# The inverse and the solve of a chunked recurrence, on 64x64 diagonal tiles of TensorE instead of zero-padded full rows

## The reference

```
for t in range(45):
    b_t = kk_t * a_t
    sa  = -S @ kk_t
    S   = S * dec_t[None, :] + outer(sa, b_t) + outer(v_t, k_t)
    o_t = S @ r_t
```

## Time and profile before

| | us |
|---|---|
| median of 3 runs | 312.54 |
| range of the runs | 311.07 to 313.73 |
| the profiled execution, its time | 310.39 |
| its span, first to last instruction | 308.6 |
| PE busy | 281.8 |
| ACT busy | 200.1 |
| DVE busy | 189.0 |
| POOL busy | 127.5 |

### The profile page before, as it was taken

The page is one execution under the profiler, slowest core; times in us unless marked ns, Lnnn a source line. Parts: engine busy times, 40 slices in busy tenths (PEclk is TensorE's granted clock), DMA queues, the critical chain, the costliest instruction groups (busy, mean ns, idle before and its releaser), DMA issues.

```text
span 308.6 us, 13595 instructions
## 1 busy us (share of the span) xinstructions
PE 281.8 (91%) x5880; PEld 214.8 (70%) x5880; DVE 189.0 (61%) x346; ACT 200.1 (65%) x356; POOL 127.5 (41%) x122
## 2 busy tenths in 40 slices
PE   3999789999999999999777886999999999999996
PEld 1557567888975666766443474887989888976785
DVE  5258878899347763424797988789765655244202
ACT  1587983555575978787998976294865326666541
POOL 9006899131040066666346159674378200021000
PEclk9999999999995999999999979999999999999999
DMA  7932221222212222221200000000000000000002
GB/s 237 415 87 62 66 57 54 62 63 63 64 54 57 62 54 63 60 62 56 62 24 0 2 2 2 2 5 4 4 4 4 4 4 5 4 4 2 2 26 74
DMA packets 20563, 14.99 MB, mean 49 GB/s; under 512 B 2328, under 2 KB 19352, under 8 KB 20376
## 3 DMA queue, kind: packets, MB, share of 16 engines
q1 hardware_dynamic: 20504, 14.13, 14.7%
HBM read 13.38 MB, written 0.74 MB: 46 GB/s over the span
## 4 chain that ended last, share of the span: by engine, by line
PE 68%; ACT 21%; DVE 6%; POOL 3%; issue 2%; DVEq 0%; POOLq 0%
PE PS L772 62%; PE PS L884 5%; ACT L342 3%; ACT arena L372 3%; ACT arena L368 2%; ACT arena L366 2%; ACT arena L407 2%; DVE PS L510 1%; ACT arena L415 1%; ACT arena L381 1%; DVE arena L670 1%; ACT arena L358 1%; POOL arena L322 1%; ACT arena L419 1%; POOL arena L326 1%
## 5 line engine op out<-in xcount | busy, mean ns | idle before, releaser
L772 PE MATMUL PS<-arena,K 64*64 64x180 f32 (+3 forms) x1296 | 132.0, 372 | 14.3 <-DVE PS L510 5.3
L772 PEld LDWEIGHTS PS<-arena,K 128*64 128x64 f32 (+2 forms) x1296 | 74.6, 145 | 55.2 <-issue 21.1
L772 PE MATMUL PS<-arena 128*45 128x45 f32 (+5 forms) x3584 | 108.1, 222 | 5.0 <-POOL arena L315 2.6
L772 PEld LDWEIGHTS PS<-arena 128*45 128x45 f32 (+3 forms) x3584 | 98.9, 125 | 18.9 <-issue 5.1
L305 POOL TENSOR_TENSOR arena<-arena 128x360 f32<-128x360 f32 x32 | 29.8, 958 | 37.8 <-DVE arena L684 37.8
L684 DVE TENSOR_TENSOR arena<-PS,arena 128x360 f32<-128x360 f32 x32 | 16.8, 531 | 23.0 <-PE PS L772 20.0
L407 ACT ACTIVATE arena<-PS,K 128x720 f32<-128x720 f32 x32 | 25.2, 861 | 2.4 <-PE PS L772 1.8
L281 POOL TENSOR_TENSOR WG<-WG,K 128x2048 f32<-128x2048 f32 x4 | 15.2, 3814 | 25.6 <-DMA WG<-wr 25.6
L559 DVE TENSOR_TENSOR arena<-PS,arena 128x360 f32<-128x360 f32 x20 | 10.6, 531 | 22.0 <-ACT arena L368 22.0
L389 ACT COPY arena<-PS 128x720 f32<-128x720 f32 x16 | 12.4, 775 | 15.4 <-PE PS L884 15.2
L772 PE MATMUL PS<-K,arena 128*45 128x64 f32 (+4 forms) x472 | 19.3, 230 | 1.9 <-DVE arena L737 0.9
(11 more groups left out here) (125 smaller groups left out, 375.3 us busy)
## 6 DMA issues: line engine op xcount, KB each, us to landing
WG<-wr SPq DMA_DIRECT2D x64, 64.0 KB, 1.9
arena<-wr SPq DMA_DIRECT2D x64, 64.0 KB, 1.8
arena<-xT SPq DMA_DIRECT2D x4, 368.0 KB, 5.0
K<-consts SPq DMA_DIRECT2D x1, 1171.0 KB, 10.2
K<-consts SPq DMA_DIRECT2D x1, 852.0 KB, 8.0
out<-arena SPq DMA_DIRECT2D x4, 180.0 KB, 1.9
K<-consts SPq DMA_DIRECT2D x1, 510.0 KB, 6.0
K<-consts SPq DMA_DIRECT2D x1, 352.0 KB, 6.8
```

The costliest lines, as they stand in the source:

```text
L772: return nc.tensor.matmul(o, l, r, start=start, stop=stop)
```

## The change

- The matmuls of `lx`, `lt`, `u`, `y2`, `o` read only the 45 rows of their own sequence, on partitions 64j to 64j+44, for both operands; `z` reads 32 rows and `w` 13 (from partition 64j+32).
- The zeroed copies go, with their waits (`ltb`, `ttb`, `lt32`, `sab`): all of ACT's share of `m`, of the last `lt` and of `w`, one of ACT's two copies in `vt`, DVE's second operation in `w`. `lx` writes 360 elements a row.
- The ones beside V are written by POOL at the outset, in two small memsets for each chunk, each behind a wait on POOL's own semaphore; ACT's and DVE's copies in `v` go.
- `TABLE` is another order of the same steps, from the first to the last. Parts of it, old and new, are shown.
- The constants lose 187 columns of 128.

```diff
@@ the table, attention's start @@
-mean.1:2 q.0:0 var.1:12 mean.1:3 k.0:0 q.0:12 var.1:3 kx.0:0 k.0:1 v.0:0 q.0:3 kx.0:1 k.0:2 v.0:1 k.0:3 kx.0:2 v.0:2
-kx.0:3 v.0:3 s.0:01 e.0:0 s.0:23 e.0:1 t.0:0 e.0:2 t.0:1 pv.0:0 t.0:2 pv.0:1 e.0:3 s.1:01 t.0:3 e.1:0 pv.0:23 t.1:0
+var.1:12 mean.1:3 k.0:0 q.0:1 var.1:3 q.0:2 kx.0:0 k.0:1 kx.0:1 q.0:3 k.0:23 v.0:0 kx.0:2 v.0:1 s.0:0 e.0:0 v.0:2
+kx.0:3 s.0:1 t.0:0 e.0:1 v.0:3 s.0:2 pv.0:0 t.0:1 s.0:3 pv.0:1 s.1:01 e.0:2 e.1:0 e.0:3 e.1:1 t.0:2 t.1:0 t.0:3 pv.1:0
@@ the table, from the first kb on @@
-ab.0:0 mean.3:3 aw.0:1 gh.0:0 ab.0:1 gg.0:0 gh.0:1 kk.0:0 gg.0:1 kk.0:1 bon.0:0 kb.0:0 bon.0:1 var.3:3 vw.0:2
-mixes.0:3 m.0:0 aw.0:2 m.1:0 kb.0:1 rk.0:3 vt.0:0 ab.0:2 vw.0:3 lx.0:0 m.0:1 lt.0:0 aw.0:3 lx.1:0 m.1:1 gh.0:2 lt.1:0
...
-lx.1:2 vt.0:3 o.0:0 lt.1:2 mean.4:0 lx.0:3 u.0:1 var.4:0 lt.0:3 lx.2:2 y2.0:1 lx.1:3 lt.2:2 lt.1:3 lx.3:2 z.0:1 lx.2:3
-lt.3:2 lt.2:3 ro.0:0 u.0:2 lx.3:3 w.0:1 mean.5:0 y2.0:2 lt.3:3 z.0:2 o.0:1 u.0:3 w.0:2 var.5:0 y2.0:3 mean.4:1 o.0:2
-var.4:1 z.0:3 mean.4:2 f.0:0 w.0:3 var.4:2 r.0:0 o.0:3 ro.0:12 mean.4:3 mean.5:12 var.4:3 var.5:12 r.1:0 ro.0:3 f.0:1
+rk.0:1 vw.0:01 aw.0:0 mixes.0:2 cb.7:3 aw.0:1 ab.0:0 y.7:3 rk.0:2 ab.0:1 gh.0:01 gg.0:0 kk.0:0 gg.0:1 kk.0:1 bon.0:0
+kb.0:0 mean.3:3 bon.0:1 kb.0:1 var.3:3 vw.0:2 m.0:01 mixes.0:3 aw.0:2 m.1:0 rk.0:3 ab.0:2 m.1:1 vt.0:0 gh.0:2 vw.0:3
...
+w.0:1 ro.0:0 lt.1:3 mean.5:0 lx.2:23 o.0:1 var.5:0 mean.4:1 lt.2:23 f.0:0 lx.3:23 lt.3:23 var.4:1 u.0:23 y2.0:23
+z.0:23 w.0:23 o.0:23 mean.4:2 ro.0:1 var.4:2 mean.4:3 mean.5:1 r.0:0 var.4:3 var.5:1 ro.0:2 r.1:0 mean.5:2 f.0:1
@@ GpSimd, for each chunk @@
                 g.memset(a(c, VD_, PP * 2 * NKV * 18), 0.0).then_inc(sem["init"], 1)
+                pool.wait_ge(sem["init"], 3 * c + 1)
+                for hh in range(2):
+                    if hh:
+                        pool.wait_ge(sem["init"], 3 * c + 2)
+                    ones = a(c, VD_, PP * 2 * NKV * 18, 64 * hh, 64 * hh + T).rearrange("q (x u) -> q x u", u=18)
+                    g.memset(ones[:, :, 9 * hh + HD], 1.0).then_inc(sem["init"], 1)
+                pool.wait_ge(sem["init"], 3 * c + 3)
@@ ScalarE @@
-                    s.copy(ones, vec("tok")[64:128, :].broadcast_to([64, PP * 2 * NKV]))
-                elif name == "m":
-                    act.wait_ge(sem["m_ev"], n)
-                    p0, p1 = i * PP // 2, (i + 1) * PP // 2
-                    for j in range(2):
-                        last = s.activation(pair(a(c, LT_[j]))[:, p0:p1], m2(c)[:, p0:p1], ACT.Copy, scale=vec(f"tok{j}"))
-                    last.then_inc(sem["ltb"], 1)
-                    for j in range(2):
-                        last = s.activation(a(c, VT_[j], 512), bank(c, 0, 512), ACT.Copy, scale=vec(f"tok{j}"))
-                    last.then_inc(sem["vt"], 1)
+                    s.copy(a(c, VT_, 512), bank(c, 0, 512)).then_inc(sem["vt"], 1)
-                elif name == "lt" and i == len(LEVELS) - 1:
-                    act.wait_ge(sem["t_ev"], n)
-                    for j in range(2):
-                        last = s.activation(pair(a(c, TB_[j])), ...)
-                    last.then_inc(sem["ttb"], 1)
-                    for j in range(2):
-                        last = s.activation(pair(a(c, LT_[j])), m2(c), ACT.Copy, scale=vec(f"early{j}"))
-                    last.then_inc(sem["lt32"], 1)
-                    s.activation(a(c, U_, 512), bank(c, 0, 512), ACT.Copy, scale=k("row32")).then_inc(sem["z_ev"], 1)
-                elif name == "w":
-                    act.wait_ge(sem["sa"], 2 * n - 1)
-                    s.activation(a(c, SA_[0], 512), a(c, Y_, 512), ACT.Copy, scale=vec("tok0")).then_inc(sem["sab"], 1)
+                    s.copy(a(c, U_, 512), bank(c, 0, 512)).then_inc(sem["z_ev"], 1)
@@ VectorE @@
-                    v.tensor_tensor(x.rearrange("q j (p t) -> q j p t", t=T),
-                                    pair(bank(c, 0)).unsqueeze(1).broadcast_to([128, 2, PP, T]),
-                                    level.unsqueeze(2).broadcast_to([128, 2, PP, T]), ALU.mult).then_inc(sem["x_ev"], 1)
+                    v.tensor_tensor(pair(a(c, X_)), pair(bank(c, 0)), over_pairs(k("levels", i * T, (i + 1) * T)),
+                                    ALU.mult).then_inc(sem["x_ev"], 1)
-                    dve.wait_ge(sem["sa"], 2 * n - 1)
-                    v.tensor_scalar(a(c, SA_[1], 512), a(c, Y_, 512), vec("tok1"), None, ALU.mult).then_inc(sem["sa"], 1)
@@ TensorE @@
+            def seq(j, lo=0, hi=T):
+                return 64 * j + lo, 64 * j + hi
-                        last = mm(to_bank(c, 0, T, j, p, T), a(c, LT_[j] + p * T, T), tt(c, p, 0))
+                        last = mm(to_bank(c, 0, T, j, p, T), m4(c, p, 2, seq(j)), tt(c, p, 0, seq(j)))
...
+                        early = seq(j, 0, 32)
+                        last = mm(to_bank(c, 0, D, j, p, T), m4(c, p, 2, early), a(c, Y_ + p * D, D, *early))
...
+                        late = seq(j, 32, T)
+                        last = mm(to_bank(c, 1, D, j, p, T), tt(c, p, 1, late), a(c, U_ + p * D, D, *late))
```

More of the change, by code:

```diff
@@ L26 @@
 GROUPS = [
-    [("tokA", 64), ("tokB", 64), ("mean", 128), ("cent", 128), ("vecs", 36)],
+    [("tokA", 64), ("tokB", 64), ("mean", 128), ("cent", 128), ("vecs", 30)],
     [("wq", 128), ("wqr", 128), ("wk", 128), ("wkr", 128), ("wv", 2 * NKV * HD), ("cosq", T), ("sinq", T),
@@ L63 @@
 HA = 4
[L64 to L68, removed]
+M4_, L_, TT_, U_, Y_ = slot(11), slot(9), slot(3), slot(19), slot(5)
+KR_, X_, VT_ = slot(1), slot(5), slot(1)
 WG1_ = slot(19) + PP * D
@@ L96 @@
[L96 to L100, removed]
@@ L111 @@
-mean.5:3 f.0:2 r.0:1 var.5:3 fo.0:0 r.0:2 f.0:3 r.1:1 r.0:3 r.1:23 fo.0:123
+tok.0:012 mean.0:01 var.0:0 mean.0:2 tok.0:3 var.0:1 mean.1:0 mean.0:3 var.0:2 var.1:0 mean.1:1 var.0:3 mean.1:2 q.0:0
+var.1:12 mean.1:3 k.0:0 q.0:1 var.1:3 q.0:2 kx.0:0 k.0:1 kx.0:1 q.0:3 k.0:23 v.0:0 kx.0:2 v.0:1 s.0:0 e.0:0 v.0:2
+kx.0:3 s.0:1 t.0:0 e.0:1 v.0:3 s.0:2 pv.0:0 t.0:1 s.0:3 pv.0:1 s.1:01 e.0:2 e.1:0 e.0:3 e.1:1 t.0:2 t.1:0 t.0:3 pv.1:0
+pv.0:23 s.1:2 e.1:2 s.1:3 e.1:3 s.2:0 t.1:12 e.2:0 pv.1:1 t.1:3 pv.1:23 s.2:123 e.2:12 t.2:012 pv.2:01 e.2:3 pv.2:2
@@ new lines @@
+t.2:3 s.3:012 e.3:0 pv.2:3 e.3:1 t.3:0 e.3:2 t.3:1 pv.3:01 attT.0:01 wo.0:0 s.3:3 wo.0:1 e.3:3 mean.2:0 t.3:2 mean.2:1
+var.2:0 t.3:3 pv.3:23 var.2:1 attT.0:23 wo.0:23 mean.2:23 var.2:23 gate.0:0123 top2.0:0 hid.0:012 hid.1:0 hid.0:3
+hid.1:123 cwT.0:012 cw2.0:01 cwT.0:3 b2.0:01 cw2.0:2 cb.0:0 cw2.0:3 b2.0:2 cb.0:1 b2.0:3 y.0:0 cb.1:0 y.0:1 cb.0:23
+cb.1:1 y.0:2 cb.1:2 hid.2:012 y.1:0 cb.2:0 y.1:1 cb.2:1 y.0:3 cb.1:3 y.1:2 cb.2:2 hid.3:01 hid.2:3 y.2:0 cb.3:0 y.2:1
+y.1:3 cb.3:1 cb.2:3 hid.4:0 hid.3:23 hid.4:1 y.2:2 cb.3:2 y.3:0 cb.4:0 y.3:1 cb.4:1 hid.4:2 hid.5:01 y.2:3 cb.3:3
@@ new lines @@
+y.4:0 cb.5:0 y.4:1 hid.4:3 hid.6:0 y.3:2 cb.5:1 cb.4:2 y.3:3 y.5:0 cb.6:0 hid.6:1 hid.7:0 hid.5:2 y.5:1 cb.4:3 y.6:0
+y.4:2 cb.6:1 cb.5:2 hid.5:3 hid.7:1 hid.6:2 y.4:3 cb.5:3 cb.7:0 y.7:0 y.5:2 cb.6:2 y.6:1 cb.7:1 hid.7:2 hid.6:3 y.7:1
+y.6:2 mean.3:0 cb.7:2 y.7:2 y.5:3 var.3:0 mean.3:12 cb.6:3 var.3:1 hid.7:3 mixes.0:0 rk.0:0 mixes.0:1 var.3:2 y.6:3
+rk.0:1 vw.0:01 aw.0:0 mixes.0:2 cb.7:3 aw.0:1 ab.0:0 y.7:3 rk.0:2 ab.0:1 gh.0:01 gg.0:0 kk.0:0 gg.0:1 kk.0:1 bon.0:0
+kb.0:0 mean.3:3 bon.0:1 kb.0:1 var.3:3 vw.0:2 m.0:01 mixes.0:3 aw.0:2 m.1:0 rk.0:3 ab.0:2 m.1:1 vt.0:0 gh.0:2 vw.0:3
@@ new lines @@
+lx.0:0 gg.0:2 lt.0:0 kk.0:2 lx.1:0 bon.0:2 kb.0:2 vt.0:1 lt.1:0 aw.0:3 m.0:2 lx.0:1 lx.2:0 ab.0:3 m.1:2 lt.0:1 lt.2:0
+lx.1:1 gh.0:3 lt.1:1 lx.3:0 gg.0:3 kk.0:3 lt.3:0 lx.2:1 bon.0:3 vt.0:2 kb.0:3 lt.2:1 lx.0:2 u.0:0 m.0:3 lt.0:2 m.1:3
+y2.0:0 lx.1:2 lx.3:1 z.0:0 vt.0:3 w.0:0 lt.3:1 o.0:0 u.0:1 lx.0:3 mean.4:0 y2.0:1 lt.0:3 var.4:0 z.0:1 lx.1:3 lt.1:2
+w.0:1 ro.0:0 lt.1:3 mean.5:0 lx.2:23 o.0:1 var.5:0 mean.4:1 lt.2:23 f.0:0 lx.3:23 lt.3:23 var.4:1 u.0:23 y2.0:23
+z.0:23 w.0:23 o.0:23 mean.4:2 ro.0:1 var.4:2 mean.4:3 mean.5:1 r.0:0 var.4:3 var.5:1 ro.0:2 r.1:0 mean.5:2 f.0:1
@@ L112 @@
+ro.0:3 var.5:2 fo.0:0 mean.5:3 r.0:1 var.5:3 f.0:2 r.1:1 f.0:3 r.0:23 r.1:23 fo.0:123
 """
@@ L1127, in shape_constants @@
     z["eye2"] = np.concatenate([r == t, r == t], 1)
-    z["levels"] = np.concatenate([(r // (2 * b) == t // (2 * b)) & (r // b > t // b) & (r < T) & (q[:, None] // 64 == j)
-                                  for b in LEVELS for j in range(2)], 1)
-    z["row32"] = r >= 32
+    z["levels"] = np.concatenate([(r // (2 * b) == t // (2 * b)) & (r // b > t // b) & (r < T) for b in LEVELS], 1)
     out = {n: np.asarray(x, np.float32) for n, x in z.items()}
@@ L1182 @@
     cst["b2"], cst["Rb"] = b2, rb
-    vecs = np.zeros((128, 36), np.float32)
+    vecs = np.zeros((128, 30), np.float32)
     cols = dict(tok_b=inp["L0_tok_b"], gamma=inp["L0_tok_gamma"], beta=inp["L0_tok_beta"], b_w=inp["L1_attn_b_w"],
@@ L1202 @@
     vecs[:, VECS.index("rb_low")] = -1.0 * (row // (NR + 1) >= 2)
-    for j in range(2):
-        for n, rows in (("feat", D), ("tok", T), ("early", 32)):
```

(1 more changed line is left out.)

62 lines of the change are left out of this document (20 added, 42 removed).

## The result

The changed kernel takes 323.37 us (median of 4 runs, 322.63 to 324.16) against 313.13 us of before in the same comparison, a ratio of 1.0385 (95% interval 1.0347 to 1.0422). It is slower, and the prediction of 308.8 us, with all of its range, missed it. The profiled execution took 323.88 us, its span is 322.1 us. Ratios leave out the runs that lie over 1.5% above the quickest of the same kernel; where a kernel spread too much for a ratio, I give its range.

The account below looks back on a forecast made before the run. The prediction took PE to bound the kernel after the ramp up to 190 us. Its terms, 0 + 0.8 - 1.2 - 2.2 - 1.1 = -3.7 us, gave 308.8 us against a median of 312.54, range 304.5 to 314.8 us.

Parts of the forecast that it names:

- Attention's start: Up to attention's first scores: ACT's four copies of ones leave the path, -1.2 us; reordering there counted as 0.
- The rest of the redrawing: First layer norms, experts, last layers: same steps, PE full, so 0, bounds -1.5 and +1.5 us.
- changes of shape: PE switching array shape between steps: 0.11 us each, 144 changes before and 151 after, +0.8 us in sum.
- The tiles themselves: PE's passes in inverse and solve: fewer rows keep the same pace, 0, bounds -3.7 us and 0.
- second rival: Inverse and solve on PE: diagonal tiles run quicker, -3.7 us more, 305.1 us in all; chance 0.06.
- Inverse and solve: Dropped ACT copies and shorter DVE `lx` evacuation (L744), counted only where the chain shows them: -2.2 us, bounds 0 and -4.
- `kb.0:1`: Ramp before the first `m`: POOL does `kb.0:1` earlier, so `m.0:1` waits less; -1.1 us, bounds -2.2 and +1.
- first rival: PE's full queue hides shorter evacuations; only shape changes and perhaps the ones copies count: 312.7 us, chance 0.21.
- fourth rival: Tail, `lx.2` to `o.0` of chunks 2 and 3: bare pairs make PE wait, 5.6 us, 314.4 us; chance 0.13.

Follow-up runs that it names:

- 4: The changed code with the new order up to `gate.0:3` and the old order behind it; 319.63 us, ratio 1.0287 to the kernel before.
- 1: The changed code with the old order of all steps; 309.19 us, ratio 0.9942 to the kernel before.
- 8: Kernel 4 with the first score of each row subtracted in attention in place of DVE's maximum; 311.54 us, ratio 0.9959 to the kernel before.
- 5: Kernel 3 with `z` and `w` reading 64 rows of each tile, not 32 and 13; 307.9 us, ratio 0.9893 to the kernel before.
- 3: The changed code with the old order up to `gate.0:3` and the new order behind it; 308.78 to 320.21 us, median 316.51.
- 6: Kernel 3 with `lx`, `lt`, `u`, `y2` and `o` reading 64 rows, not 45; 307.62 to 313.48 us in 4 runs.
- 2: The code of before, with its zeroed copies and full rows, in the new order; 331.12 us, ratio 1.0640 to the kernel before.
- 13: The changed code in the old order, with the new order only between `gate.0:3` and `o.0:0`; 309.94 us, ratio 0.9981 to the kernel before.

## Why the prediction was wrong

**The step that failed** is attention behind its start, which stands at nothing in the sum. "Attention's start" ends with the first scores, and of all else in the order "The rest of the redrawing" says: "the steps are the same, ... and PE was full there. 0, bounds -1.5 and +1.5". Under the changes of shape, attention's steps of one kind that "now stand together" even count as most of a gain of 1.3 us. The order costs 10.4 us there (4 against 1): from `s.1:0` to `gate.0:3` PE idles 8.5 us and not 0.5, and most of it goes when DVE's maximum is made short (8). That PE was full under the old order says that the old order kept it full. DVE was busy 29.67 of 36.80 us in that stretch, four fifths. The trace of before shows it for the stretch from 20 to 60 us too (DVE busy 33.08 of 40.00 us), but the earlier trace rows, from which I reasoned, begin at 178 us:

```profile
20.00:60.00 40.00, 35.98 (x790) 27.92 (x789) 33.08 (x62) 29.75 (x53) 27.81 (x28) 1.00 0.22 61
```

With so little slack on DVE, scores that are put together make the transposes wait.

**The clock** is a term that the prediction doesn't have. The time at half clock went from 10.2 to 27.3 us. Three of the stretches lie among or right behind gaps of PE, one of them in attention; the one at 279.4 doesn't. From `o.0:2` to `mean.5:1` after needs 11.2 us, and 5, with the same passes in the same order and no fall, 6.9: the fall costs 4.3 us.

**The sum of the profiles.** The 13.5 us between the spans are +9.9 for attention (`q.0:0` to `gate.0:3`), +3.0 from there to `m.0:0`, +1.1 from `m.0:0` to `fo.0:3`, and -0.5 ahead of `q.0:0`. The 3.0 us go with the clock: after has 10.4 us at half clock in them, and 3, with the same code and order there, has 3.9 and needs 3.4 us less. The 1.1 us are the fall in the tail less what the change won: 5 and 6, without the fall, need 124.6 and 124.7 us there, before 126.5.

**The tiles themselves, 0:** right, and the second rival was wrong. The passes run at the old pace; the timeline of PE, after:

```profile
205.53 1.56 PE L742 MATMUL PS<-arena 45*45 45x45 f32 x64
207.02 0.83 PE L742 MATMUL PS<-arena,K 128*64 128x360 f32 x4
...
263.86 2.92 PE L742 MATMUL PS<-arena 45*45 45x45 f32 x128
266.71 0.88 PE L742 MATMUL PS<-arena,K 64*128 64x360 f32 x4
```

64 passes of `lt` hand over in 1.49 us to a step of another shape (1.50 before). The row of 128 passes is two steps: 1.39 us in front of its own shape (1.39 before) and 1.46 in front of another.

**Changes of shape, 0.11 us each:** by the distances of starts in after, away from waits and half clock, seven steps of 64 `lt` passes take 1.35 to 1.39 us in front of a step on 45 rows, and five take 1.43 to 1.49 in front of another. That bears it out. What I hadn't looked at: in the old order the tail (`o.0:0` to `fo.0:3`) grew from 69.1 to 70.5 us with the new tiles (1; 70.0 to 71.6 in the seven others that have this tail), and the 128-row steps between the new tiles are now of another shape. In 5 and 6, in the new order, it is 69.5 and 69.0. The changes of shape as the cause of that difference weren't tried by themselves.

**Attention's start, -1.2 us:** `q.0:0` to `s.1:0` went from 24.7 to 24.0 us with the changed code in the old order (1). So the mechanism was right, and the term nearly twice too large. The new order adds nothing to it: its 24.1 (after) and 24.2 us (2) lack `t.0:2`, which takes about 1.0 us behind `s.1:0`. POOL's memsets take 0.24 us each and are hidden, inside the bounds.

**Inverse and solve, -2.2, and `kb.0:1`, -1.1:** L744's successor takes what was predicted, by the groups of DVE:

```profile
L717 DVE TENSOR_TENSOR arena<-PS,K 128x360 f32<-128x360 f32 x16 | 8.4, 528 | 6.3 <-PE PS L742 5.9
```

DVE was rid of 5.4 us in all, where some 8 were forecast. `m.0:0` to `o.0:0` shrank by 1.2 us with the changed code (57.4 to 56.2 in 1) and by 0.7 more with the order (55.5 in 3), where 3.3 were forecast; but the tail behind it grew by 1.4 in 1, so that in the old order nothing is left of the two terms in the profiles (126.5 and 126.7 us from `m.0:0` to `fo.0:3`). As a whole, 1 is 0.6% or 1.9 us quicker than before (309.19 to 311.09): 0.7 us are attention's start, and 1.0 us lies between `gate.0:3` and `m.0:0` in the profiles, where before has 6.8 us at half clock and 1 none. So in the old order the first rival holds (PE's pace hides it); in the new one the same code is worth 7.7 us (2 against after), which no term foresaw. `m.0:1` did start early (3.0 us behind `m.0:0`, before 13.2), and 13 shows that this is worth nothing. PE's idle time from the first `m` to the last `o` is 1.3 us, as I said (below 3.5), and the time did not follow it.

**The fourth rival** put the loss on the pairs of chunks in the tail, at waits between them. There are none: PE is full in 272.0 to 279.4. The place was right and the mechanism wrong. (With the old code such waits exist: in 2 PE idles 4.2 us from `o.0:0` to `fo.0:3`.)
